# W_in centred and row sums scaled when added; every second tile of x read as columns from a second, transposed layout

## The chip, the core and the metric

The kernel runs on one core of a Trainium2 chip. The metric is the device time of one execution in microseconds (us). Before: median 858.76 us of three runs (858.76, 859.01, 854.37).

## What is computed

With `ln` a layer norm without weights and `rms(v, g)` = v / sqrt(mean(v^2) + 1e-5) * g:

```
h  = rms(ln(x), g_res) @ W_in.T + b_in
x1 = x + h + depool(rms(ctx, g_init)[:, :512])[plug]
y  = x1 + gelu(ln(x1) @ w1 + b1) @ w2 + b2
```

x is 4096 x 512, ctx 3202 x 1024, w1 512 x 2048, all fp32. `depool` is a first-order recurrence over the rows of the context (a scan); `plug` picks a scanned row for each row of x and is worked out from the mask by integer sums.

## The kernel before

The rows of x are 32 tiles of 128 rows; four tiles make a group of 512 rows (8 groups). Each fp32 product is formed as three fp32r products of high and low parts (`split_product`, L780 to L783): hi\*hi, hi\*lo, lo\*hi. A high part is a ScalarE copy into fp32r, a low part the difference of the value and its high part.

**First stage**, one tile after another (`t` from 0 to 31 on every engine). SyncE loads the tile into one of 16 slots (`xa`). VectorE takes its statistics (`tile_stats`, L927, L928), POOL turns them into scale and bias (`scales`, L470 to L473), ScalarE normalizes (`tile_norm`, L634, into `n_rows`), TensorE transposes in four pieces (`transpose_first`, L776) into one of three PSUM banks, ScalarE forms the high part (`tile_high`, L641), VectorE the low part (`tile_low`, L932), and TensorE multiplies with W_in (`project`, 12 matmuls of 128x512). VectorE adds the product to x in the slot (`tile_add`, L938), and SyncE stores x1 to memory (`store_x1`, L359). High and low parts have four slots (`HB`), the products three banks. W_in is split once at the start, scaled by g_res (`high_w_in`, `low_w_in`).

Between the tiles, at slots written out by hand (`if t == ...`), stand the integer work on the mask (`mask_parts` to `mask_rows`, `one_hots_p`, `one_hots_q`, `count_rows`, `finish_plug` on VectorE; `mask_totals`, `count_positions`, `count_before` on TensorE), the first two blocks of the context scan (`squares`, `times_g_init`, `scale_rows`, `scan_row`, `carry` L800, `add_carry`), which are stored in a table in memory, and for group 0 the reload of x1 (`x_next`), `add_bias`, the gathers from the table (`add_context`, L510) on POOL, the second layer norm (`second_stats`, `group_scale`, `second_norm` L1057) and its transposes (`transpose_second`, L824). POOL forms the low parts of w1 and w2 (`low_w1` L478, `low_w2` L484).

**Second stage**, 8 groups: for m from 0 to 15, `ffn1` (12 matmuls), twice Gelu on ScalarE, the low part on VectorE (L1144) and two steps later `ffn2` (12 matmuls); the scan blocks 2 to 6 and the preparation of the next group lie beside it. Each engine executes its own instructions in the order in which they are written; semaphores connect them.

## Time and profile before

| | |
|---|---|
| timed runs | 858.76, 859.01, 854.37 us; median 858.76 |
| the profiled execution | 854.02 us |
| its span, first to last instruction | 851.9 us |
| TensorE matmul busy | 827.5 us, 97% of the span, 3758 instructions |
| VectorE, ScalarE, POOL busy | 315.2, 293.1, 267.8 us |
| moved by DMA | 73.17 MB |
| granted TensorE clock, mean | 0.998 |

The page cuts the span into 40 slices of 21.3 us; TensorE is at nine tenths or more in all but the first and the last two or so. In rows of the profile PE is TensorE, PEld its weight loads, DVE VectorE, ACT ScalarE, POOL GpSimd; SPq and ACTq are the queues on which SyncE and ScalarE issue DMAs. A busy time of a matmul overlaps the next one's; steps from start to start tell its length better.

### The profile page before, as it was taken

Reading aid. Unit: us, or ns where it says so; the run is one execution under the profiler, and the core shown is the slowest. Engines: PE = TensorE matmul, PEld = TensorE weight load, DVE = VectorE, ACT = ScalarE, POOL = GpSimd, SP = SyncE. Lnnn points to the kernel's source line nnn. Section 1 sums busy time; section 2 is a strip of 40 time slices with the busy share of each in tenths; the row PEclk is TensorE's granted clock in tenths of the full one; section 3 lists DMA queues with packets and bytes.
Section 4 is the critical chain, followed back from the end, with each engine's and each line's share of the span. In section 5 each row is a group of like instructions: output and inputs, shape, how many; then the busy total and the mean of one; then the engine's idle time right before and its main releaser. Section 6 shows DMA issues by size and latency. Waiting matters only on the chain.

```text
span 851.9 us, 10840 instructions
## 1 busy us (share of the span) xinstructions
PE 827.5 (97%) x3758; PEld 679.9 (80%) x3758; DVE 315.2 (37%) x523; ACT 293.1 (34%) x506; POOL 267.8 (31%) x290
## 2 busy tenths in 40 slices
PE   4998999999999999999999999999999999999998
PEld 3776788788888888888888887888888888888886
DVE  5888862444342242414151424234113311241112
ACT  4674535542532235222622243223222322222221
POOL 6263666970162005310522044202500250011000
PEclk9999999999999999999999999999999999999999
DMA  9876798160214212241125021402300140010001
GB/s 235 278 212 189 249 240 307 50 165 7 75 50 122 49 49 74 72 99 38 43 82 132 0 74 49 97 0 95 53 1 1 50 89 9 0 49 1 1 1 49
DMA packets 35688, 73.17 MB, mean 86 GB/s; under 512 B 5796, under 2 KB 5796, under 8 KB 33768
## 3 DMA queue, kind: packets, MB, share of 16 engines
q1 hardware_dynamic: 26972, 61.54, 22.1%
q0 software_dynamic: 4608, 8.39, 6.2%
q10 hardware_dynamic: 4080, 2.89, 1.2%
q8 instruction: 14, 0.23, 0.1%
q14 instruction: 14, 0.11, 0.0%
HBM read 48.92 MB, written 23.89 MB: 85 GB/s over the span
## 4 chain that ended last, share of the span: by engine, by line
PE 86%; DVE 4%; POOL 4%; issue 2%; ACT 2%; DMA 1%; SPq 0%; POOLq 0%; DVEq 0%; ACTq 0%
PE acc L781 14%; PE acc L782 14%; PE acc L783 14%; PE h_bank L781 13%; PE h_bank L783 13%; PE h_bank L782 13%; PE t_bank L824 2%; DVE cl L944 1%; PE t_bank L776 1%; DMA x_next<-x_part 1%; POOL w_lo L478 1%; POOL cl L497 1%; POOL w_lo L484 1%; POOL x_next L505 1%; DMA xa_even<-in_x_dram 1%
## 5 line engine op out<-in xcount | busy, mean ns | idle before, releaser
L1144 DVE TENSOR_TENSOR h_lo<-g_f,h_hi 128x512 fp32r<-128x512 f32 x128 | 100.9, 788 | 452.0 <-ACT g_f L728 452.0
L726 ACT ACTIVATE h_hi<-h_bank,b_c 128x512 fp32r<-128x512 f32 x128 | 88.1, 688 | 434.4 <-PE h_bank L783 429.6
L781 PE MATMUL h_bank<-xt_hi,w_hi 128*128 128x512 f32 x512 | 201.9, 394 | 0.0
L781 PE MATMUL acc<-w_hi,h_hi 128*128 128x512 f32 x512 | 199.8, 390 | 0.0
L783 PE MATMUL h_bank<-xt_hi,w_lo 128*128 128x512 f32 x512 | 199.4, 389 | 0.0
L782 PE MATMUL h_bank<-xt_lo,w_hi 128*128 128x512 f32 x512 | 199.3, 389 | 0.0
L783 PE MATMUL acc<-w_hi,h_lo 128*128 128x512 f32 x512 | 199.2, 389 | 0.0
L782 PE MATMUL acc<-w_lo,h_hi 128*128 128x512 f32 x512 | 199.2, 389 | 0.0
L782 PEld LDWEIGHTS h_bank<-xt_lo,w_hi 128*128 128x128 f32 x512 | 96.2, 188 | 20.8 <-issue 1.2
L781 PEld LDWEIGHTS h_bank<-xt_hi,w_hi 128*128 128x128 f32 x512 | 96.1, 188 | 20.8 <-issue 1.2
L783 PEld LDWEIGHTS h_bank<-xt_hi,w_lo 128*128 128x128 f32 x512 | 96.1, 188 | 20.1
L783 PEld LDWEIGHTS acc<-w_hi,h_lo 128*128 128x128 f32 x512 | 96.1, 188 | 20.0
L781 PEld LDWEIGHTS acc<-w_hi,h_hi 128*128 128x128 f32 x512 | 96.1, 188 | 19.7
L782 PEld LDWEIGHTS acc<-w_lo,h_hi 128*128 128x128 f32 x512 | 96.1, 188 | 19.6
L728 ACT ACTIVATE g_f<-h_bank,b_c 128x512 f32<-128x512 f32 x128 | 87.4, 683 | 0.0
L510 POOL DMA_INDIRECT x_next<-scan_table,idx x32 | 51.3, 1602 | 65.9 <-DMA scan_table<-cl 55.9
L497 POOL TENSOR_TENSOR cl<-cl,g_init_b 128x512 f32<-128x512 f32 x24 | 31.3, 1313 | 97.2 <-ACT ch L646 96.9
L571 POOL TENSOR_TENSOR x_cur<-x_next,b_b 128x512 f32<-128x512 f32 x32 | 43.5, 1390 | 56.3 <-DMA out_dram<-x_cur 55.9
L515 POOL TENSOR_SCALAR va_b<-mv_b 128x4 f32<-128x4 f32 x8 | 1.6, 196 | 187.2 <-DVE mv_b L1048 187.2
L505 POOL TENSOR_TENSOR x_next<-x_next,b_in_b 128x512 f32<-128x512 f32 x32 | 46.3, 1446 | 33.8 <-DMA x_next<-x_part 30.2
L781 PE MATMUL acc<-win_hi,h_hi 128*128 128x512 f32 x88 | 38.1, 434 | 0.0
L783 PE MATMUL acc<-win_hi,h_lo 128*128 128x512 f32 x88 | 34.9, 396 | 0.0
(145 smaller groups left out, 706.3 us busy)
## 6 DMA issues: line engine op xcount, KB each, us to landing
x_next<-x_part SPq DMA_DIRECT2D x8, 1024.0 KB, 4.8
out_dram<-x_cur SPq DMA_DIRECT2D x32, 256.0 KB, 2.1
w_raw<-in_L_ffn_w_dram SPq DMA_DIRECT2D x6, 1024.0 KB, 9.0
scan_table<-cl SPq DMA_DIRECT2D x6, 896.0 KB
ch<-in_ctx_dram SPq DMA_DIRECT2D x20, 256.0 KB, 2.9
cl<-in_ctx_dram SPq DMA_DIRECT2D x5, 1024.0 KB
xa_even<-in_x_dram SPq DMA_DIRECT2D x16, 256.0 KB, 5.2
xa_odd<-in_x_dram SPq DMA_DIRECT2D x16, 256.0 KB, 5.7
```

What stands on the lines that cost most here:

```text
L478: pool.tensor_tensor(w_lo[:, k, r], w_raw[:, k, r], w_hi[:, k, r].bitcast(F32), ALU.subtract).then_inc(w1_ready, 1)
L497: pool.tensor_tensor(rows[:, j, :], rows[:, j, :], g_init_b[:], ALU.mult).then_inc(g_scaled, 1)
L505: step(pool.tensor_tensor(x_next[:, i, :], x_next[:, i, :], b_in_b[:], ALU.add))
L510: pool.indirect_dma_start(x_next[:, i, :], None, rows, bass.IndirectOffsetOnAxis(ap=idx[:, i:i + 1].bitcast(U32), axis=0), compute_op=ALU. ...
L571: ins = pool.tensor_tensor(x_cur[:, i, :], x_next[:, i, :], b2_b[:], ALU.add)
L726: act.activation(h_hi[:, m % HB, :], h_bank[m % 2][:], ACT.Gelu, bias=b1_c[:, m:m + 1])
L728: act.activation(g_f32[:], h_bank[m % 2][:], ACT.Gelu, bias=b1_c[:, m:m + 1]).then_inc(gelu_done, 1)
L781: nc.tensor.matmul(dst, a_hi, b_hi, start=first, stop=False)
L782: nc.tensor.matmul(dst, a_hi, b_lo, start=False, stop=False)
L783: return nc.tensor.matmul(dst, a_lo, b_hi, start=False, stop=final)
L824: ins = nc.tensor.transpose(t_bank[i % 2][:, k * P:(k + 1) * P], n_rows[:, i, k * P:(k + 1) * P], ident[:])
L1144: dve.tensor_tensor(h_lo[:, m % HB, :], g_f32[:], h_hi[:, m % HB, :].bitcast(F32), ALU.subtract).then_inc(h_split, 1)
```

## The change

1. **Normalization moves behind the product.** TensorE transposes x as it was loaded. W_in is scaled by g_res and each column is centred: four plain fp32 matmuls (`sum_w_in`) with `g_wide`, a 128-column copy of g_res, give the column sums in every row of a bank, and VectorE subtracts 1/512 of them (`centre_w_in`). The product is scaled by the row's factor when it is added (`tile_add` becomes a `scalar_tensor_tensor`). `tile_norm` and two of POOL's four scale operations go.
2. **Odd tiles from 3 on** (15 of 32) are not transposed. The host passes `x_cols`, x with rows and columns of each tile exchanged; SyncE loads it beside the tile into an unused part of `w_raw` (`xc`, 12 slots). Their low part is formed on POOL (`tile_low`).
3. **Around it**: the first four x1 tiles stay in `x_next` and are neither stored nor loaded again; POOL's `add_bias`, gathers, `low_w1`, half of `low_w2` and `group_scale` for group 0 get slots between the tiles; POOL's two clearings of `cl` and `ch_all` go to VectorE; two of the four W_in loads are issued by ScalarE; on TensorE `mask_totals`, `count_before` and the first carry come one tile earlier, and on VectorE most of the mask work and parts of the scan too.

```diff
@@ -95,7 +95,17 @@
-def xattn_ffn(nc, x, ctx, mask, w_in, b_in, g_res, g_init, w1, b1, w2, b2, out):
+def from_host(t):
+    return t % 2 == 1 and t >= 3
+TURNED = [t for t in range(NT) if not from_host(t)]
+HOSTED = [t for t in range(NT) if from_host(t)]
+XTR = 12
+def xattn_ffn(nc, x, x_cols, ctx, mask, w_in, b_in, g_res, g_init, w1, b1, w2, b2, out):
@@ -176,10 +187,28 @@
+        def xc(t):
+            u = HOSTED.index(t) % XTR
+            q = 3 - u // K
+            return w_raw[:, u % K, q * D:(q + 1) * D]
+        def turned_bank(t):
+            return first_bank[TURNED.index(t) % 3]
+        def x1(t):
+            return x_next[:, t, :] if t < TI else xa(t)
@@ -306,9 +341,9 @@
+            for k in range(2, K):
+                sp.dma_start(win_raw[:, k, :], win_v[:, k, :]).then_inc(win_loaded[k], 16)
...
-            for k in range(K):
-                sp.dma_start(win_raw[:, k, :], win_v[:, k, :]).then_inc(win_loaded[k], 16)
@@ -316,6 +351,11 @@
+                if from_host(t):
+                    m = HOSTED.index(t)
+                    if m >= XTR:
+                        wait_apart(sp, xc_lo, m - XTR + 1)
+                    sp.dma_start(xc(t), x_cols[t, :, :]).then_inc(xc_loaded[m % XTR], 16)
@@ -374,19 +414,15 @@
-                if t > 0:
+                if t > TI:
...
-                    if loaded >= XR:
+                    if XR <= loaded < XR + TI:
+                        wait_apart(sp, acc_read, loaded - XR + 1)
+                    if loaded >= XR + TI:
...
-                if t == 17:
-                    wait_apart(sp, plug_ready, 1)
-                    for j in range(TI):
-                        wait_x1(j)
-                    sp.dma_start(x_next[:], x1_dram[0, :, :, :]).then_inc(x_next_loaded, 16)
@@ -467,10 +504,14 @@
+                if t0 > 0:
+                    pool.wait_ge(ra_ready, t0)
...
-                step(pool.tensor_tensor(ra[:, u], va_a[:, 0:n], neg_half[:, 0:n], ALU.pow))
-                step(pool.tensor_tensor(mr_a[:, 0:n], mv_a[:, u, 0], ra[:, u], ALU.mult))
-                pool.tensor_scalar(na_bias[:, u], mr_a[:, 0:n], -1.0, 1.0, ALU.mult, ALU.mult).then_inc(ra_ready, n)
+                pool.tensor_tensor(ra[:, u], va_a[:, 0:n], neg_half[:, 0:n], ALU.pow).then_inc(ra_ready, n)
+            def tile_low(t):
+                pool.wait_ge(x_hi, t + 1)
+                pool.tensor_tensor(h_lo[:, t % HB, :], xc(t), h_hi[:, t % HB, :].bitcast(F32), ALU.subtract).then_inc(xc_lo, 1)
@@ -515,41 +556,47 @@
-            pool.memset(cl[:], 0.0).then_inc(zeroed, 1)
-            pool.memset(ch_all[:], 0.0).then_inc(zeroed, 1)
-            for t in range(4):
-                scales(t, 1)
+            scales(0, 2)
+            scales(2, 2)
...
-            scales(4, 2)
...
+                if t + 2 < NT and from_host(t + 2):
+                    tile_low(t + 2)
...
-                if t == 18:
-                    pool.wait_ge(plug_ready, 1)
-                    gather_indices(0)
-                    pool.wait_ge(x_next_loaded, 16)
-                    for i in range(TI):
-                        add_bias(i)
-                if t % 2 == 0 and t + 6 < NT:
-                    scales(t + 6, 2)
+                if t % 4 == 2 and t + 2 < NT:
+                    scales(t + 2, TI)
...
-            wait_apart(pool, table_stored, STORED + BLOCK_STORED * 2)
-            for i in range(TI):
-                add_context(0, i, 2)
-            for k in range(K):
-                low_w1(0, k, 1)
-            group_scale(0)
+                if 14 <= t <= 17:
+                    pool.wait_ge(acc_read, t - 13)
+                    add_bias(t - 14)
+                if t == 18:
+                    pool.wait_ge(plug_ready, 1)
+                    gather_indices(0)
+                if t in (23, 24):
+                    if t == 23:
+                        wait_apart(pool, table_stored, STORED + BLOCK_STORED * 2)
+                    add_context(0, 2 * (t - 23), 2)
+                    add_context(0, 2 * (t - 23) + 1, 2)
+                if t in (25, 26):
+                    low_w1(0, 2 * (t - 25), 1)
+                    low_w1(0, 2 * (t - 25) + 1, 1)
+                if t == 27:
+                    low_w2(0, 0, 2)
+                    low_w2(0, 1, 2)
+                if t == 28:
+                    group_scale(0)
...
-            for q in range(4):
+            for q in range(2, 4):
@@ -622,23 +671,19 @@
-            def tile_norm(t):
-                act.wait_ge(ra_ready, t + 1)
-                if t >= TI:
-                    act.wait_ge(t_done, t - TI + 1)
-                u = t % XR
-                act.activation(n_rows[:, t % TI, :], xa(t), ACT.Identity, bias=na_bias[:, u:u + 1],
-                               scale=ra[:, u:u + 1]).then_inc(n_ready, 1)
...
-                act.wait_ge(t_done, t + 1)
...
-                act.activation(h_hi[:, t % HB, :], first_bank[t % 3][:], ACT.Copy).then_inc(t_hi, 1)
+                if from_host(t):
+                    m = HOSTED.index(t)
+                    act.wait_ge(xc_loaded[m % XTR], 16 * (m // XTR) + 16)
+                    act.activation(h_hi[:, t % HB, :], xc(t), ACT.Copy).then_inc(x_hi, 1)
+                else:
+                    act.wait_ge(x_turned, TURNED.index(t) + 1)
+                    act.activation(h_hi[:, t % HB, :], turned_bank(t)[:], ACT.Copy).then_inc(x_hi, 1)
@@ -654,34 +699,28 @@
-            def high_w_in(k):
+            for k in range(K):
+                act.activation(g_wide[:, k, :], ones[:], ACT.Copy, scale=g_res_c[:, k:k + 1]).then_inc(g_made, 1)
+            for k in range(K):
...
-                act.activation(win_hi[:, k, :], win_raw[:, k, :], ACT.Copy, scale=g_res_c[:, k:k + 1]).then_inc(win_hi_done, 1)
-            high_w_in(0)
-            high_w_in(1)
-            tile_norm(0)
-            high_w_in(2)
+                act.activation(win_g[:, k, :], win_raw[:, k, :], ACT.Copy, scale=g_res_c[:, k:k + 1]).then_inc(win_scaled, 1)
...
-            high_w_in(3)
-            tile_norm(1)
+            for k in range(K):
+                act.wait_ge(win_centred, k + 1)
+                act.activation(win_hi[:, k, :], win_raw[:, k, :], ACT.Copy).then_inc(win_hi_done, 1)
...
-            tile_norm(2)
...
-                if t + 3 < NT:
-                    tile_norm(t + 3)
@@ -769,13 +808,21 @@
-                pe.wait_ge(n_ready, t + 1)
-                if t >= 3:
-                    pe.wait_ge(t_lo, t - 2)
+                pe.wait_ge(xa_loaded[t % XR], 16 * (t // XR) + 16)
+                n = TURNED.index(t)
+                if n >= 3:
+                    pe.wait_ge(x_lo, n - 2)
...
-                    ins = nc.tensor.transpose(first_bank[t % 3][:, k * P:(k + 1) * P],
-                                              n_rows[:, t % TI, k * P:(k + 1) * P], ident[:])
-                ins.then_inc(t_done, 1)
+                    ins = nc.tensor.transpose(turned_bank(t)[:, k * P:(k + 1) * P], xa(t)[:, k * P:(k + 1) * P], ident[:])
+                ins.then_inc(x_turned, 1)
+            def sum_w_in():
+                for k in range(K):
+                    pe.wait_ge(g_made, k + 1)
+                    pe.wait_ge(win_loaded[k], 16)
+                    ins = nc.tensor.matmul(acc[3][:], g_wide[:, k, :], win_raw[:, k, :], start=(k == 0), stop=(k == K - 1))
+                ins.then_inc(win_summed, 1)
@@ -783,7 +830,10 @@
-                pe.wait_ge(t_lo, t + 1)
+                if from_host(t):
+                    pe.wait_ge(xc_lo, HOSTED.index(t) + 1)
+                else:
+                    pe.wait_ge(x_lo, TURNED.index(t) + 1)
@@ -819,26 +869,27 @@
+            sum_w_in()
...
-            for t in range(3):
-                project(t)
-                transpose_first(t + 2)
-            for t in range(3, NT):
-                if t + 2 < NT:
+            for t in range(NT):
+                if t + 2 < NT and not from_host(t + 2):
...
-                if t == 3:
+                if t == 2:
...
+                if t == 14:
+                    count_before()
...
-                    count_before()
-                if t == 16:
@@ -928,14 +981,16 @@
-                dve.wait_ge(t_hi, t + 1)
-                dve.tensor_tensor(h_lo[:, t % HB, :], first_bank[t % 3][:], h_hi[:, t % HB, :].bitcast(F32),
-                                  ALU.subtract).then_inc(t_lo, 1)
+                dve.wait_ge(x_hi, t + 1)
+                dve.tensor_tensor(h_lo[:, t % HB, :], turned_bank(t)[:], h_hi[:, t % HB, :].bitcast(F32),
+                                  ALU.subtract).then_inc(x_lo, 1)
...
-                dve.tensor_tensor(xa(t), p_bank[t % 3][:], xa(t), ALU.add).then_inc(acc_read, 1)
+                dve.wait_ge(ra_ready, t + 1)
+                u = t % XR
+                dve.scalar_tensor_tensor(x1(t), p_bank[t % 3][:], ra[:, u:u + 1], xa(t), ALU.mult, ALU.add).then_inc(acc_read, 1)
@@ -1014,13 +1069,18 @@
-            def low_w_in(ks):
-                dve.wait_ge(g_res_loaded, 16)
-                for k in ks:
-                    dve.wait_ge(win_hi_done, k + 1)
-                    dve.scalar_tensor_tensor(win_lo[:, k, :], win_raw[:, k, :], g_res_c[:, k:k + 1], win_hi[:, k, :].bitcast(F32),
-                                             ALU.mult, ALU.subtract).then_inc(win_lo_done, 1)
+            def centre_w_in(k):
+                if k == 0:
+                    dve.wait_ge(win_summed, 1)
+                dve.wait_ge(win_scaled, k + 1)
+                dve.scalar_tensor_tensor(win_raw[:, k, :], acc[3][:], -1.0 / D, win_g[:, k, :], ALU.mult, ALU.add)\
+                    .then_inc(win_centred, 1)
+            def low_w_in(k):
+                dve.wait_ge(win_hi_done, k + 1)
+                dve.tensor_tensor(win_lo[:, k, :], win_raw[:, k, :], win_hi[:, k, :].bitcast(F32),
+                                  ALU.subtract).then_inc(win_lo_done, 1)
@@ -1050,63 +1110,64 @@
-            low_w_in((0, 1))
-            tile_stats(1)
-            low_w_in((2,))
...
-            low_w_in((3,))
-            tile_stats(2)
-            tile_stats(3)
+            centre_w_in(0)
+            centre_w_in(1)
+            low_w_in(0)
+            centre_w_in(2)
+            low_w_in(1)
+            centre_w_in(3)
+            low_w_in(2)
+            low_w_in(3)
...
-            tile_stats(4)
-            tile_stats(5)
+            for t in range(1, 6):
+                tile_stats(t)
...
@@ -1203,8 +1264,11 @@
+    laid = dict(inputs)
+    laid['L0_xattn_W_in'] = _np.asarray(inputs['L0_xattn_W_in']).T
+    laid['x_cols'] = _np.asarray(inputs['x']).reshape(NG, P, TI, K, P).transpose(0, 2, 4, 3, 1).reshape(NT, P, D)
...
-        a = _np.ascontiguousarray(inputs[name].T if name == 'L0_xattn_W_in' else inputs[name])
+        a = _np.ascontiguousarray(laid[name])
...
```

TensorE's order at the start, before (`n_rows` are the normalized rows, `win_hi` and `win_lo` the parts of W_in):

```order
L776 MATMUL t_bank<-ident,n_rows 128x128 [waits n_ready,consts_made]
L776 MATMUL t_bank<-ident,n_rows 128x128 x3
L776 MATMUL t_bank<-ident,n_rows 128x128 [waits n_ready]
L776 MATMUL t_bank<-ident,n_rows 128x128 x3
L781 MATMUL acc<-win_hi,h_hi 128x512 [waits win_lo_done,win_hi_done,t_lo]
L782 MATMUL acc<-win_lo,h_hi 128x512
L783 MATMUL acc<-win_hi,h_lo 128x512
L781 MATMUL acc<-win_hi,h_hi 128x512 [waits win_lo_done,win_hi_done]
```

and with the change (`g_wide` is g_res over 128 columns):

```order
L816 MATMUL t_bank<-ident,xa_even 128x128 [waits xa_loaded0,consts_made]
L816 MATMUL t_bank<-ident,xa_even 128x128 x3
L824 MATMUL acc<-win_raw,g_wide 128x512 [waits win_loaded0,g_made]
L824 MATMUL acc<-win_raw,g_wide 128x512 [waits win_loaded1,g_made]
L824 MATMUL acc<-win_raw,g_wide 128x512 [waits win_loaded2,g_made]
L824 MATMUL acc<-win_raw,g_wide 128x512 [waits win_loaded3,g_made]
L816 MATMUL t_bank<-ident,xa_even 128x128 [waits xa_loaded1]
L816 MATMUL t_bank<-ident,xa_even 128x128 x3
L816 MATMUL acc<-ident,xa_even 128x128 [waits xa_loaded2]
L816 MATMUL acc<-ident,xa_even 128x128 x3
L828 MATMUL acc<-win_hi,h_hi 128x512 [waits win_lo_done,win_hi_done,x_lo]
L829 MATMUL acc<-win_lo,h_hi 128x512
```

The transposes wait for a load instead of normalized rows; four fp32 products stand between tile 0 and tile 1, and tile 2 is transposed ahead of the first product.

VectorE's order from the low part of tile 0 (L985; L1077 centres, L1082 forms the low part of W_in, L980 and L981 are the statistics) to the second of the five statistics, with the change:

```order
L985 TENSOR_TENSOR h_lo<-t_bank,h_hi 128x512 [waits x_hi]
L1077 SCALAR_TENSOR_TENSOR win_raw<-acc,win_g 128x512 [waits win_scaled,win_summed]
L1077 SCALAR_TENSOR_TENSOR win_raw<-acc,win_g 128x512 [waits win_scaled]
L1082 TENSOR_TENSOR win_lo<-win_raw,win_hi 128x512 [waits win_hi_done]
L1077 SCALAR_TENSOR_TENSOR win_raw<-acc,win_g 128x512 [waits win_scaled]
L1082 TENSOR_TENSOR win_lo<-win_raw,win_hi 128x512 [waits win_hi_done]
L1077 SCALAR_TENSOR_TENSOR win_raw<-acc,win_g 128x512 [waits win_scaled]
L1082 TENSOR_TENSOR win_lo<-win_raw,win_hi 128x512 [waits win_hi_done] x2
L985 TENSOR_TENSOR h_lo<-t_bank,h_hi 128x512 [waits x_hi]
L980 BN_STATS st_a<-xa_even 128x6 [waits xa_loaded1]
L981 BN_AGGR mv_a<-st_a 128x2 [waits dve_self]
```

All that concerns W_in waits for `win_summed`, TensorE's sums. Three more statistics follow, then the low part of tile 2 and the mask's work. Before, the same stretch was:

```order
L1022 SCALAR_TENSOR_TENSOR win_lo<-win_raw,g_res_c,win_hi 128x512 [waits win_hi_done,g_res_loaded]
L1022 SCALAR_TENSOR_TENSOR win_lo<-win_raw,g_res_c,win_hi 128x512 [waits win_hi_done]
L927 BN_STATS st_a<-xa_even 128x6 [waits xa_loaded1]
L928 BN_AGGR mv_a<-st_a 128x2 [waits dve_self]
L1022 SCALAR_TENSOR_TENSOR win_lo<-win_raw,g_res_c,win_hi 128x512 [waits win_hi_done,g_res_loaded]
L932 TENSOR_TENSOR h_lo<-t_bank,h_hi 128x512 [waits t_hi]
L1022 SCALAR_TENSOR_TENSOR win_lo<-win_raw,g_res_c,win_hi 128x512 [waits win_hi_done,g_res_loaded]
L927 BN_STATS st_a<-xa_even 128x6 [waits xa_loaded2]
L928 BN_AGGR mv_a<-st_a 128x2 [waits dve_self]
L927 BN_STATS st_a<-xa_even 128x6 [waits xa_loaded3]
L928 BN_AGGR mv_a<-st_a 128x2 [waits dve_self]
L932 TENSOR_TENSOR h_lo<-t_bank,h_hi 128x512 [waits t_hi]
```

There, two statistics stand between the low part of W_in and that of tile 1, and two more before that of tile 2.

POOL's order from the gathers of group 0 (L551) to the scale of the group (L557), with the change (L514 is the low part of a tile from the host, L519 and L525 those of w1 and w2):

```order
L551 DMA x_next<-scan_table,idx 128x512 [waits table_stored]
L551 DMA x_next<-scan_table,idx 128x512 x3
L514 TENSOR_TENSOR h_lo<-w_raw,h_hi 128x512 [waits x_hi]
L519 TENSOR_TENSOR w_lo<-w_raw,w_hi 128x512 [waits w_hi_done] x2
L509 TENSOR_SCALAR va_a<-mv_a 128x4 [waits mv_a_ready,ra_ready]
L510 TENSOR_TENSOR ra<-va_a,neg_half 128x4 [waits pool_self]
L519 TENSOR_TENSOR w_lo<-w_raw,w_hi 128x512 [waits w_hi_done] x2
L514 TENSOR_TENSOR h_lo<-w_raw,h_hi 128x512 [waits x_hi]
L525 TENSOR_TENSOR w_lo<-w_raw,w_hi 128x512 [waits w_hi_done] x2
L556 TENSOR_SCALAR va_b<-mv_b 128x4 [waits mv_b_ready]
L557 TENSOR_TENSOR rb<-va_b,neg_half 128x4 [waits pool_self]
L514 TENSOR_TENSOR h_lo<-w_raw,h_hi 128x512 [waits x_hi]
```

The low parts of tiles 27, 29 and 31 (L514) now stand between the gathers and the other work; before, POOL did only scale and bias for the tiles, and the gathers came behind the last of them.

## Rows read from the trace of the kernel before

**Rows 1.** Stretches: us, busy time and instructions of each engine, clock, DMA share, GB/s.

```profile
26.50:130.60 104.10, 98.57 (x505) 79.78 (x504) 82.55 (x170) 55.87 (x99) 55.55 (x85) 0.98 0.76 230
...
209.90:299.80 89.90, 89.85 (x402) 73.93 (x402) 29.93 (x44) 30.04 (x56) 26.17 (x23) 1.00 0.24 70
...
60.00:80.00 20.00, 16.83 (x76) 12.77 (x75) 14.81 (x35) 10.69 (x19) 9.87 (x19) 0.91 0.72 217
```

**Rows 2.** Timeline of TensorE: start, us, engine, line, operation.

```profile
26.56 0.47 PE L781 MATMUL acc<-win_hi,h_hi 128*128 128x512 f32 x1
...
130.62 0.39 PE L781 MATMUL h_bank<-xt_hi,w_hi 128*128 128x512 f32 x1
...
133.34 0.39 PE L781 MATMUL h_bank<-xt_hi,w_hi 128*128 128x512 f32 x1
```

**Rows 3.** Chain of waits, in order of time: start us, us, what.

```profile
74.42 1.11 PE t_bank L776 x4
75.53 1.71 PE acc L800 x2
...
107.50 0.44 PE t_bank L776 x4
110.71 0.44 PE t_bank L776 x4
...
255.32 0.86 PE t_bank L800 x2
```

**Rows 4.** Timeline of TensorE: its waits in the projection [idle before <-releaser].

```profile
56.88 0.66 PE L776 MATMUL acc<-ident,n_rows 128*128 128x128 f32 x4 [1.69 <-ACT n_rows L634]
...
74.42 1.11 PE L776 MATMUL t_bank<-ident,n_rows 128*128 128x128 f32 x4 [2.92 <-ACT n_rows L634]
...
97.67 0.66 PE L776 MATMUL t_bank<-ident,n_rows 128*128 128x128 f32 x4 [0.67 <-ACT n_rows L634]
```

**Rows 5.** VectorE, one line each: count, min/median/max ns, first and last start.

```profile
L944 DVE SCALAR_TENSOR_TENSOR cl<-cl x18: 683/1666/1787, 65.5 to 523.9; 128x512 f32<-128x512 f32 x18
...
L938 DVE TENSOR_TENSOR xa_even<-acc,xa_even x11: 657/658/692, 20.3 to 101.4; 128x512 f32<-128x512 f32 x11
```

**Rows 6.** Timeline of the start: VectorE, and issues on ScalarE's queue.

```profile
5.32 0.69 DVE L927 BATCH_NORM_STATS2 st_a<-xa_even 128x6 f32<-128x512 f32 x1 [4.31 <-DMA xa_even<-in_x_dram]
...
8.86 0.70 DVE L927 BATCH_NORM_STATS2 st_a<-xa_even 128x6 f32<-128x512 f32 x1 [0.39 <-DMA xa_even<-in_x_dram]
...
11.97 0.35 ACTq L675 DMA_DIRECT2D g_init_b<-in_L_xattn_g_init_dram  x1
...
12.61 0.69 DVE L927 BATCH_NORM_STATS2 st_a<-xa_even 128x6 f32<-128x512 f32 x1
...
13.39 0.66 ACTq L676 DMA_DIRECT2D b_c<-in_L_ffn_b_dram  x1
...
13.50 0.66 DVE L927 BATCH_NORM_STATS2 st_a<-xa_even 128x6 f32<-128x512 f32 x1
...
22.63 0.17 DVE L960 TENSOR_SCALAR part_i<-mask_i 128x26 int32<-128x26 int32 x1
...
24.23 0.17 DVE L973 COPY part_f<-cum_f 128x3 f32<-128x3 f32 x1
```

**Rows 7.** Timeline at the end of the projection: SyncE's queue, POOL, VectorE.

```profile
96.50 0.82 SPq L344 DMA_DIRECT2D scan_table<-cl_next  x2
...
104.03 1.82 POOL L510 DMA_INDIRECT x_next<-scan_table,idx  x1 [0.69 <-issue]
...
110.84 5.62 POOL L478 TENSOR_TENSOR w_lo<-w_raw,w_hi 128x512 fp32r<-128x512 f32 x4
...
121.18 1.04 POOL L516 TENSOR_TENSOR rb<-va_b,neg_half 128x4 f32<-128x4 f32 x1
...
122.32 1.92 DVE L1057 TENSOR_SCALAR n_rows<-x_next,mv_b,rb 128x512 f32<-128x512 f32 x4 [0.20 <-POOL rb L516]
```

**Rows 8.** DMA issues: KB each, us from issue to landing.

```profile
b_c<-in_L_ffn_b_dram ACTq DMA_DIRECT2D x1, 8.0 KB, 22.3
```

107 lines of the change are left out of this document (62 added, 45 removed).

## The prediction

> **What bounds the kernel now.** I read the stretches first. In a feed-forward group TensorE is busy 89.85 of 89.90 us; the projection of the first 32 tiles, 26.5 to 130.6 us, has 98.57 of 104.10 [rows 1]. So time can be won where the projection waits, where TensorE does work that can be left out, or in the start; the feed-forward groups keep all their matmuls.
>
> Then TensorE's timeline [rows 2] and the chain of waits [rows 3]. Twelve matmuls, one tile's product, take 133.34 - 130.62 = 2.72 us. A tile with its four transposes takes 110.71 - 107.50 = 3.21 us. The transposes cost 0.49 us per tile. The projection of tile 3 begins at 26.56 and the first feed-forward matmul at 130.62: 104.1 us for 29 tiles, of which 29 x 2.72 = 78.9 are products, 26 x 0.49 = 12.7 transposes. Waits on the normalized rows take 1.7, 2.9 and 0.7 us [rows 4]. Behind the second one the granted clock is low (0.91 over 60 to 80 us [rows 1], its lower level of 1.2 GHz for part of that stretch): the carry there takes 1.71 where another takes 0.86, and the four transposes 1.11 where others take 0.44 [rows 3, 4]. That is 1.5 us more, so the waits cost 5.3 + 1.5 = 6.8 us. The rest of the 104.1, some 5.7 us, is the first transposes of the feed-forward, the carries and counts.
>
> **The change, part by part.**
>
> *Transposes.* Of the 26 sets issued after the projection of tile 3, thirteen go (tiles 7, 9, ... 31): 13 x 0.49 = 6.4 us on the bounding engine. The transposes that stay read x as loaded, so statistics, scales and normalization no longer stand ahead of them. All three long waits name the normalized rows [rows 4]; I take all 6.8 us as gained and nothing, if another wait follows in their place, as the lower end. What is late next is the high and low parts, which need one ScalarE pass and one VectorE or POOL pass, with three tiles of lead; and the addition, which now needs the scale. VectorE loses 15 low-part subtractions, about 0.66 us each by the nearest operation of that shape with one operand in PSUM [rows 5], so it has more air; ScalarE loses 32 passes. That is hidden either way, and worth nothing beyond the waits. The store and reload of the first four x1 tiles go too: they were beside other work.
>
> Together: -6.4 - 6.8 = **-13.2 us** between the projection of tile 3 and the feed-forward.
>
> *Start.* This part gets dearer. The first load landed at 5.3 us and the sixth at 8.9, so 0.7 us each [rows 6]. Tile 0 is now about third of five loads on two queues: 6.7 to 7.3, I take 7.0. Its transposes take 1.1 us at the lower clock [rows 3]. Then come four plain fp32 products of W_in with a row of g: 0.86 us each at 2.4 GHz, 1.71 at 1.2 GHz, by the carry, the same kind and size [rows 3]. The bounds are 3.4 and 6.8; I take two at either level, 5.1, and reach 13.2. Only then can VectorE centre the four pieces and form their low parts: eight operations of 0.6 to 0.7 us, one ScalarE pass exposed at the end, 5.5 us: 18.7. ScalarE issues four small loads before the high part of tile 1: from 11.97 to 14.05, 2.1 us [rows 6]. They begin at about 17.4, so that high part ends near 20.1 and the low part near 20.8.
>
> Behind it VectorE now has five statistics before the low part of tile 2: 5 x 0.89 (13.50 - 12.61) = 4.5. With the low part 25.9, and with the mask's integer work, which TensorE now needs one tile earlier and which takes 24.4 - 22.6 = 1.8 us [rows 6], 27.6. TensorE, done with tile 1 near 23.5, waits some 4 us, longer than the 2.9 us behind which the clock fell above; so I add 1.5 us as there. The product of tile 3 begins at 27.8 + 2.7 + 1.5 = 32.0, against 26.56: **+5.4 us**. Lower end +3 (all sums at 2.4 GHz, clock kept), upper end +8 (all at 1.2 GHz, loads 1 us later).
>
> *POOL at the end of the projection.* POOL executes in order, and the low parts of the tiles from the host stand between its gathers and the low parts of w1 and w2. The table's last store was issued by 97.3, and the first gather began at 104.03: 6.7 us at most [rows 7]. The second block's carry is placed as before, so the store goes at about 90 and gathers begin by 96.5, four in 6.8 us (104.03 to 110.84) until 103.3. A subtraction takes 5.62 / 4 = 1.4 [rows 7]: the low part of tile 27 is there at 104.7, its product due at 32.0 + 24 x 2.72 + 12 x 0.49 + 3 = 106. Four subtractions for w1, four scales and tile 29 come next: 104.7 + 5.6 + 1.2 + 1.4 = 112.9, due at 111.9: 1 us late. Two more subtractions, then the scale of the group (1.4 us from 120.83 to 122.2), then the first normalized row (1.92 / 4) [rows 7]: 117.6, where TensorE, 1 us behind already, wants it at 115.6: 3 us late in all. But 6.7 us is an upper bound, since POOL had other work between that store and its gather; with a table 2 us sooner 1 us is left, with one 3 us sooner nothing, and where POOL meets VectorE at the port 4 us. I take the middle of 3 and 1, **+2.0 us**, bounds 0 and 4.
>
> *The port.* The same VectorE operation on two SBUF operands takes 683 ns at least and 1666 ns at the median [rows 5]; most of the slow ones lie in the groups in which POOL forms low parts of the weights. The additions, with one operand in PSUM, take 657 to 692 ns throughout [rows 5]; they and the low parts, of the same kind, are most of what VectorE does here. The Trainium skill, "SBUF — State Buffer", section "SBUF: two separate sides", says that a VectorE instruction with two SBUF inputs and a POOL instruction hold the shared port in turn, each for its whole length; it speaks against putting subtractions on POOL. By that rule the six scan rows behind tiles 12 to 16, which met no POOL work before, may each wait. The sum takes nothing for it; the third case below does.
>
> Sum: -13.2 + 5.4 + 2.0 = **-5.8 us**. Against the profiled execution, 854.02 us with a span of 851.9, that is 848.2. The three timed runs have a median of 858.76, and of the four executions two are near 854 and two near 859. I expect the same spread after, so I start from the mean of the four, 856.5, and forecast **851 us** (856.5 - 5.8 = 850.7).
>
> **The cases.**
>
> 1. *The sum holds*, -4.3 to -8: 0.52.
>
> 2. *The start costs less*: the clock stays up and the sums end sooner, +3, and POOL is in time, 0: -10.2 us, 846. For it: behind the wait of 1.7 us the four transposes took 0.66 us and not the 1.11 they took behind 2.9 us [rows 4], so the clock holds through the shorter kind. Against it: five statistics stand ahead of tile 2 whatever the clock does. 0.15.
>
> 3. *The port and POOL give back the gain.* Six scan rows of 1.67 instead of 0.68 are 6 us on VectorE between tiles 12 and 16, with about 3 us of lead: TensorE waits 3 us more at the two carries. That gives -2.8, or 854, within 0.5% (4.3 us, about what a measurement of this kernel can tell from no change). For it: the spread in [rows 5], and POOL's 15 new subtractions. Against it: they meet only where both happen to run. 0.20.
>
> 4. *Slower: POOL blocked by a small load.* From tile 5 on POOL waits for four small loads before it scales the context. The last one took 22.3 us from its issue [rows 8]; issued near 19 instead of 13.4 it lands at 41. Behind that wait stand two context rows, four scales and the low part of tile 9: 5.2 us, 46.5, due at about 50. So it decides from a landing at 45 on, and one at 58, if 15 extra loads on the other queue hold it back, would cost 13 us: -5.8 + 13 = +7, or 864. Against it: the extra loads of that time are 1.5 MB less the 1 MB of x1 stores that go. With any other cause of a gain turned into a loss above 4.3 us it gets 0.13.
>
> So faster 0.67, same 0.20, slower 0.13. The range: 844 is case 2 with the lower two executions of four; 858 takes in the worst ends of case 3 and leaves out case 4: 0.8 inside.
>
> **What would show it.** In the profile after: twelve-matmul tiles alternate 2.72 and 3.21 us with no wait over 1 us from tile 3 to 26; the first matmul of tile 3 lies near 32 us, behind a wait of some 4 us on the mask's totals or the low part of tile 2; a wait of 1 to 3 us before the transposes of the feed-forward, released by POOL or by the normalized rows; feed-forward groups of 89.9 us as before; the first feed-forward matmul near 124.8. I am wrong if that matmul comes after 128, or if TensorE waits for the low parts of tiles from the host before tile 27. If the feed-forward groups change length, the sum is wrong at a place that it holds fixed.

## The result, and the profile after

The changed kernel takes 860.97 us (median of 12 runs, 857.82 to 863.14), the kernel before 856.24 us in the same comparison: ratio 1.0051, 95% interval 1.0036 to 1.0067. It is 4.7 us or 0.5% slower; the forecast was 851 us, and 860.97 lies above its range of 844 to 858.

The profiled execution took 862.8 us with a span of 861.0, against 854.02 and 851.9 before. This pair lies further apart than the medians: 862.8 is among the longest executions after, 854.02 is shorter than any of the twelve before. Four marks on TensorE's timeline cut the 9.1 us between these two into pieces:

| from the span's start, us | before | after | longer by |
|---|---|---|---|
| product of tile 3 begins | 26.56 | 33.58 | +7.0 |
| from there to the product of tile 26 | 84.35 | 75.52 | -8.8 |
| from there to the first feed-forward matmul | 19.71 | 28.77 | +9.1 |
| from there to the end of the span | 721.3 | 723.1 | +1.8 |

So the middle gained as it should in kind, the start cost about what was expected, and 9 us were lost between tile 26 and the feed-forward, where the forecast had 1.0 (2.0 for POOL, less two sets of transposes).

The stretches of the kernel after (stretch: us, then busy time and instructions of PE, PEld, DVE, ACT, POOL, then granted clock, DMA share, GB/s):

```profile
33.50:137.80 104.30, 94.73 (x451) 75.96 (x451) 82.55 (x154) 35.99 (x72) 64.80 (x61) 0.97 0.74 227
219.10:309.00 89.90, 89.83 (x403) 73.90 (x402) 30.14 (x44) 29.99 (x56) 26.15 (x23) 1.00 0.24 70
20.00:40.00 20.00, 14.99 (x63) 11.71 (x62) 16.95 (x39) 4.99 (x11) 8.32 (x14) 0.91 0.87 265
40.00:60.00 20.00, 17.89 (x84) 14.22 (x83) 18.86 (x38) 11.71 (x30) 14.49 (x14) 1.00 0.51 137
60.00:80.00 20.00, 19.55 (x115) 15.83 (x115) 19.00 (x36) 9.24 (x20) 15.94 (x17) 1.00 0.93 337
80.00:100.00 20.00, 19.16 (x89) 15.20 (x88) 18.91 (x36) 6.43 (x8) 7.90 (x9) 1.00 0.80 231
```

The first two rows answer to [rows 1]. The projection is as long as before (104.3 us) with 3.8 us less of TensorE's work in it; the feed-forward group has not moved. In the third column of busy times (DVE), VectorE works 19 of every 20 us from 40 to 100. Before, the stretch from 60 to 80 had 14.81 [rows 1]. It has no air left, though it lost 15 subtractions. Before, it was nearly as full on either side of that stretch:

```profile
40.00:60.00 20.00, 18.31 (x114) 14.99 (x113) 18.30 (x34) 14.76 (x34) 12.44 (x18) 1.00 0.68 187
...
80.00:100.00 20.00, 19.34 (x95) 15.44 (x94) 18.55 (x36) 10.05 (x14) 10.10 (x20) 1.00 0.73 253
```

What TensorE waited for from 20 to 150 us (engine, tile and line, then the releaser, whose work ended the wait: us, times, longest):

```profile
PE h_bank L855 <- DVE part_f L1028: 4.2, 1, 4.2
PE acc L828 <- POOL h_lo L514: 3.7, 1, 3.7
PE t_bank L877 <- DVE n_rows L1115: 2.4, 1, 2.4
PE h_bank L828 <- DVE xa_odd L993: 1.3, 1, 1.3
PE h_bank L850 <- DVE cl_next L999: 0.8, 1, 0.8
```

The three waits of [rows 4] are gone. In their place stand the mask's totals (4.2), the low part of tile 27 on POOL (3.7), and the normalized rows of the first feed-forward group (2.4). Behind each of these three the granted clock falls to the lower level for part of the next 20 us, to a mean of 0.91, or some 1.8 us lost each time.

The chain of waits shows what stood behind the last two (start us, us, what; in order of time):

```profile
99.98 0.37 SPq L384
...
100.39 5.74 DMA scan_table<-cl_next
...
107.05 1.28 POOL x_next L551
...
112.88 1.54 POOL x_next L551
114.42 1.30 POOL h_lo L514
115.72 2.45 POOL w_lo L519 x2
...
119.64 2.51 POOL w_lo L519 x2
122.15 1.25 POOL h_lo L514
123.40 0.44 POOL w_lo L525
...
126.32 1.01 POOL rb L557
...
127.43 1.43 DVE n_rows L1115
...
128.91 1.92 PE t_bank L877 x8
```

The table's last store is issued at 99.98, where [rows 7] have 96.50, and the first gather begins at 107.05 instead of 104.03. VectorE ended its last addition of the carry at 97.03; the store came 2.9 us later because it stands in SyncE's queue behind that of an x1 tile, whose addition ended at 99.45. Before, it was 93.65, and the same 2.9 us. Behind the four gathers POOL has two low parts of tiles, six low parts of weights and two scales in one queue. TensorE is at that time waiting for POOL, not leading it.

Why VectorE is full is seen in its timeline and POOL's at the same time (start, us, engine, line, operation). VectorE:

```profile
73.67 0.68 DVE L985 TENSOR_TENSOR h_lo<-t_bank,h_hi 128x512 fp32r<-128x512 f32 x1
74.27 0.15 DVE L1096 COPY grp<-h_bank 128x8 f32<-128x8 f32 x1
74.46 0.17 DVE L1097 TENSOR_TENSOR_SCAN fa<-one_row,grp 128x8 f32<-128x8 f32 x1
74.67 1.22 DVE L1098 TENSOR_TENSOR fa<-fa,grp 128x8 f32<-128x8 f32 x1
75.92 0.16 DVE L1099 TENSOR_TENSOR fa<-fa,h_bank 128x8 f32<-128x8 f32 x1
76.12 1.22 DVE L1100 TENSOR_TENSOR plug_f<-cnt,fa 128x32 f32<-128x32 f32 x1
77.37 1.20 DVE L1101 TENSOR_SCALAR plug<-plug_f 128x32 int32<-128x32 f32 x1
```

POOL:

```profile
74.57 1.29 POOL L546 TENSOR_TENSOR x_next<-x_next,b_in_b 128x512 f32<-128x512 f32 x1
76.01 1.29 POOL L514 TENSOR_TENSOR h_lo<-w_raw,h_hi 128x512 fp32r<-128x512 f32 x1
77.25 1.29 POOL L546 TENSOR_TENSOR x_next<-x_next,b_in_b 128x512 f32<-128x512 f32 x1
```

The same three operations before (L1038, L1040, L1041 there):

```profile
74.70 0.17 DVE L1038 TENSOR_TENSOR fa<-fa,grp 128x8 f32<-128x8 f32 x1
...
75.10 0.19 DVE L1040 TENSOR_TENSOR plug_f<-cnt,fa 128x32 f32<-128x32 f32 x1
75.32 0.18 DVE L1041 TENSOR_SCALAR plug<-plug_f 128x32 int32<-128x32 f32 x1
```

Each of these operations on 8 or 32 columns starts during a POOL instruction of 1.29 us and ends when that one ends: 74.67 + 1.22 = 75.89 against 74.57 + 1.29 = 75.86. Eight operations on 8 to 32 columns took 1.2 us instead of 0.2 in the kernel after, one in the kernel before: some 7 us more on VectorE. Four of the eight met the low part of a tile (L514). The other four met POOL's multiplications with g_init (L538) and additions of b_in (L546), which the kernel before has too, at other times.

### The profile page after: what moved, and what is told of

The parts are those of the page before. It is cut to its first block, busy times and chain, and to the rows that moved or that the text cites. A ratio compares the mean times of both kernels' runs of the same rounds, so it can differ in the third digit from the quotient of the medians.

```text
span 861.0 us, 10600 instructions
## 1 busy us (share of the span) xinstructions
PE 831.4 (97%) x3706; PEld 678.6 (79%) x3706; DVE 322.4 (37%) x514; ACT 272.5 (32%) x482; POOL 270.9 (31%) x249
## 4 chain that ended last, share of the span: by engine, by line
PE 81%; DVE 10%; POOL 2%; issue 2%; DMA 2%; ACT 2%; SPq 0%; ACTq 0%; DVEq 0%; POOLq 0%
PE acc L828 13%; PE acc L829 13%; PE acc L830 13%; PE h_bank L828 13%; PE h_bank L829 13%; PE h_bank L830 13%; PE t_bank L877 2%; DVE st_a L980 2%; DVE cl L999 1%; DVE h_lo L985 1%; DMA ch<-in_ctx_dram 1%; DVE xa_even L993 1%; POOL x_next L551 1%; PE acc L824 1%; DMA scan_table<-cl_next 1%
## 5 line engine op out<-in xcount | busy, mean ns | idle before, releaser
L828 PEld LDWEIGHTS h_bank<-xt_hi,w_hi 128*128 128x128 f32 x512 | 96.5, 188 | 20.9 <-issue 1.2
L551 POOL DMA_INDIRECT x_next<-scan_table,idx x32 | 50.9, 1590 | 71.8 <-DMA scan_table<-cl 57.7
L538 POOL TENSOR_TENSOR cl<-cl,g_init_b 128x512 f32<-128x512 f32 x24 | 30.9, 1292 | 102.8 <-ACT ch L691 97.6
L546 POOL TENSOR_TENSOR x_next<-x_next,b_in_b 128x512 f32<-128x512 f32 x32 | 46.5, 1453 | 30.6 <-DMA x_next<-x_part 27.3
```

The costliest lines, as they stand in the source:

```text
L538: pool.tensor_tensor(rows[:, j, :], rows[:, j, :], g_init_b[:], ALU.mult).then_inc(g_scaled, 1)
L546: step(pool.tensor_tensor(x_next[:, i, :], x_next[:, i, :], b_in_b[:], ALU.add))
L551: pool.indirect_dma_start(x_next[:, i, :], None, rows, bass.IndirectOffsetOnAxis(ap=idx[:, i:i + 1].bitcast(U32), axis=0), compute_op=ALU. ...
L828: nc.tensor.matmul(dst, a_hi, b_hi, start=first, stop=False)
```

## The experiments

All are edits of the changed kernel, each compared with the kernel before on the same chip. The chip isn't the same for all: the medians of the kernel before lie between 855.05 and 857.31 us in these comparisons, so runs are best held against each other by their ratios. This table has the marks of the profiled executions and the ratio to the kernel before. A mark is that of one execution: with the same work ahead of it on TensorE and VectorE, tile 3 begins at 33.58 in the kernel after and at 32.33 in e1, where the four sums took 4.98 us and not 6.10.

| run | product of tile 3 | product of tile 26 | first gather | feed-forward | median us | ratio (95%) |
|---|---|---|---|---|---|---|
| before | 26.56 | 110.91 | 104.03 | 130.62 | | |
| after | 33.58 | 109.10 | 107.05 | 137.87 | 860.97 | 1.0051 (1.0036-1.0067) |
| e1_late_dve | 32.33 | 107.84 | 105.75 | 134.74 | 858.94 | 1.0032 (1.0007-1.0057) |
| e2_all_dve | 32.39 | 112.02 | 109.14 | 137.24 | 857.86 | 1.0043 (1.0019-1.0067) |
| e3_no_host | 32.82 | 109.31 | 105.75 | 133.28 | 855.82 | 1.0003 (0.9983-1.0024) |
| e4_no_centre | 23.53 | 104.40 | 101.59 | 130.81 | 854.21 | 0.9985 (0.9967-1.0004) |
| e5_early_stats | 27.41 | 102.50 | 99.94 | 130.75 | 853.68 | 0.9969 (0.9949-0.9989) |
| e6_early_late_scale | 28.34 | 103.87 | 101.28 | 128.25 | 853.35 | 0.9955 (0.9937-0.9972) |
| e7_turned_early_scale | 28.21 | 104.78 | 101.18 | 127.56 | 850.03 | 0.9920 (0.9904-0.9937) |
| e8_extra_pool | 27.05 | 105.19 | 101.77 | 128.28 | 852.28 | 0.9948 (0.9929-0.9967) |
| e9_short_turned | 27.51 | 103.98 | 96.08 | 126.34 | 850.74 | 0.9918 (0.9889-0.9946) |
| e10_short_hosted | 26.78 | 100.72 | 95.29 | 122.59 | 846.41 | 0.9868 (0.9832-0.9903) |
| e11_defer_only | 23.26 | 99.83 | 95.89 | 122.42 | 848.44 | 0.9902 (0.9865-0.9939) |
| e12_table_ahead | 27.07 | 107.55 | 100.49 | 129.40 | 851.85 | 0.9958 (0.9941-0.9974) |
| e13_gathers_between | 28.09 | 103.65 | 95.38 | 125.52 | 849.33 | 0.9915 (0.9886-0.9943) |

### e1_late_dve: the last three low parts on VectorE

```diff
+def on_pool(t):
+    return from_host(t) and t < 27
-                if t + 2 < NT and from_host(t + 2):      # POOL
+                if t + 2 < NT and on_pool(t + 2):
-                if t + 2 < NT and not from_host(t + 2):  # VectorE
+                if t + 2 < NT and not on_pool(t + 2):
```

> The changed kernel, with the low parts of tiles 27, 29 and 31 on VectorE and not on POOL (12 of 15 stay on POOL). Theory A (POOL's order at the end: these low parts stand behind the wait for the table and the four gathers): the wait of about 3.3 us ahead of the product of tile 27 and the slow clock behind it go, and the later wait gets shorter; the first feed-forward matmul comes at 130 to 132 us, not 137.9, and the time is 853 to 856 us, not 861. Rival B (the table itself is late because VectorE is behind, so the second wait, for the scale of the group, takes the whole place of the first): the first feed-forward matmul stays at 135 or later, time 858 or more.

Measured: 858.94 us. The wait of 3.7 us at tile 27 is gone, and another has grown:

```profile
PE t_bank L894 <- DVE n_rows L1132: 5.7, 1, 5.7
```

The feed-forward comes 3.1 us earlier, not 6 to 8, and 1.25 us of that were there at tile 3 already, which the edit does not touch. The time is as rival B gave it, the mark 0.3 us short of its 135. POOL's late low parts cost about 2 us; behind them stands the same chain of table, gathers, scale and normalized rows.

### e2_all_dve: all low parts on VectorE

The same edit with `on_pool` always false: POOL has no low parts of tiles.

> The changed kernel, with the low parts of all 15 tiles from the host on VectorE. Theory C (the port: VectorE's operations on 26 columns, 1.2 us instead of 0.18, sit behind POOL's subtractions): at most two of them stay above 1 us, which gives VectorE 6 to 7 us back, about what the 12 low parts before 100 us cost it; tile 26 starts at about 109 us as before, and with the waits at the end gone the time is 853 to 857 us. Rival D (these operations are slow for a cause of their own, or behind POOL's other work): at least six stay at 1.2 us, VectorE has 8 us more to do, tile 26 starts at 114 us or later, and the time stays at 860 or above.

Measured: 857.86 us, four slow small operations, gathers at 109.14. Both theories missed. VectorE got some 11 subtractions more before the table (11 x 0.6 = 6.6 us) and lost four slow operations (4 us); the gathers came 2.1 us later. VectorE's own load moves the table. The profiled execution, 862.09 us, is one of the four of ten that took over 861, so these marks are later than those of a middling one.

### e3_no_host: nothing from the second layout

```diff
 def from_host(t):
-    return t % 2 == 1 and t >= 3
+    return False
```

> The changed kernel without tiles from the host: all 32 are loaded once and transposed on TensorE, low parts on VectorE; the deferred normalization and the centred W_in stay. TensorE gets 15 x 0.49 = 7.3 us more, POOL 15 subtractions less. Theory A with C: the two waits at the end (6 us and 3 us of slow clock) go, so the time comes to 857 to 860 us. Rival D (VectorE alone is the bound from 20 to 100 us and now has 10 us more): 864 us or more.

Measured: 855.82 us, better than either theory gave and equal to the kernel before. TensorE does all 13 sets of transposes again, 6.4 us of work, and the feed-forward comes 4.6 us earlier than with the second layout. So in this order the second layout costs 4 to 5 us (1.0051 against 1.0003). Its saving is nowhere on the path, and what it put on POOL is.

### e4_no_centre: no sums, no centring

```diff
-            sum_w_in()
...
-                act.activation(win_hi[:, k, :], win_raw[:, k, :], ACT.Copy)
+                act.activation(win_hi[:, k, :], win_raw[:, k, :], ACT.Copy, scale=g_res_c[:, k:k + 1])
```

This leaves the row mean out of the normalization.

> The changed kernel without the centring of W_in: no column sums, W_in is scaled and split straight from its load (the mean of a row is not taken out of the product). Theory S (the four plain fp32 products and the chain behind them cost the start 6 to 7 us that nothing hides): the product of tile 3 begins at 26 to 28 us, not 33.6, and the time falls by 5 to 7 us to about 855. Rival E (VectorE is the bound from 20 to 100 us whatever the start does, and only its own work counts; or the wait for the table at the end takes the gain): less than 2.5 us reach the end, 858.5 or above.

Measured: 854.21 us, the time as theory S gave it, tile 3 earlier than it did (23.53, not 26 to 28). Tile 3 begins 10 us earlier, tile 26 only 4.7 us. TensorE now waits 3.5 us for VectorE's additions instead: the head start runs into VectorE's queue. This gave the next theory (V): VectorE's load from 20 us to the table sets the table, and table, gathers and scale set the feed-forward.

### e5_early_stats: VectorE's work moved into its own gap

```diff
             tile_stats(0)
+            tile_stats(1)
             tile_low(0)
+            tile_stats(2)
+            mask_parts()
             centre_w_in(0)
...
-            for t in range(1, 6):
-                tile_stats(t)
...
                 if t == 0:
-                    mask_parts()
+                    for i in range(3, 6):
+                        tile_stats(i)
```

> The changed kernel, with 4.5 us of VectorE's work (the statistics of tiles 1 and 2 and the mask's integer work) moved into the 6 us in which VectorE waits for the sums of W_in. Theory V (VectorE has no air from 20 to 105 us, so what it does there sets the table and, through the gathers, the end): the product of tile 3 begins near 27 rather than 33.6, the gathers begin near 102 rather than 107, the first feed-forward matmul comes at 131 to 134, and the time is 854 to 857. Theory R (the start is only a start: the rest of the projection waits for other things, as where the centring was left out and 10 us at tile 3 became 5 at tile 26): the gathers begin after 105, the feed-forward after 135.5, the time is 858.5 or more.

Measured: 853.68 us, 0.8% under the kernel after, with nothing else touched. VectorE at the start:

```profile
10.79 0.68 DVE L980 BATCH_NORM_STATS2 st_a<-xa_even 128x6 f32<-128x512 f32 x1
...
11.67 0.15 DVE L1015 TENSOR_SCALAR part_i<-mask_i 128x26 int32<-128x26 int32 x1
...
13.26 0.17 DVE L1028 COPY part_f<-cum_f 128x3 f32<-128x3 f32 x1
14.02 1.29 DVE L1077 SCALAR_TENSOR_TENSOR win_raw<-acc,win_g 128x512 f32<-128x512 f32 x2 [0.59 <-PE acc L824]
```

The statistics and the mask's work fit ahead of the sums' end at no cost. Everything that follows is 6 to 7 us earlier, to the gathers (99.94) and the feed-forward (130.75), each a little earlier than theory V gave it. Theory V holds, and theory R does not.

### e6_early_late_scale: late low parts on VectorE, scale ahead of the weights

On top of e5 and e1, POOL does the scale of the first group before six low parts of weights:

```diff
-                if t in (25, 26):
-                    low_w1(0, 2 * (t - 25), 1)
-                    low_w1(0, 2 * (t - 25) + 1, 1)
-                if t == 27:
-                    low_w2(0, 0, 2)
-                    low_w2(0, 1, 2)
                 if t == 28:
                     group_scale(0)
+                    for k in range(K):
+                        low_w1(0, k, 1)
+                    low_w2(0, 0, 2)
+                    low_w2(0, 1, 2)
```

> The kernel of the run before this one, with the low parts of tiles 27, 29 and 31 on VectorE, and with the scale of the first feed-forward group ahead of the six low parts of weights on POOL. Theory P (at the end the chain is gathers, statistics, scale, normalization, and each subtraction that stands in POOL's queue between gathers and scale makes it longer): the wait on the normalized rows, 5.7 us with the late low parts alone on VectorE, falls under 3, the first feed-forward matmul comes 2 to 4 us earlier than without this, and the time is 851 to 854. Theory Q (the landing of the gathers sets the statistics, whatever POOL does behind them): the scale comes less than 1 us earlier against the landing of the fourth gather, and the time is 855 or more.

Measured: 853.35 us. The feed-forward comes 2.5 us before that of e5, as theory P had it, but the longest wait on the normalized rows is 3.2 us. POOL now stands idle before the scale, and VectorE before the last statistics:

```profile
107.11 1.54 POOL L568 DMA_INDIRECT x_next<-scan_table,idx  x1 [0.30 <-issue]
...
115.74 0.20 POOL L573 TENSOR_SCALAR va_b<-mv_b 128x4 f32<-128x4 f32 x1 [5.63 <-DVE mv_b L1123]
```

```profile
114.60 0.69 DVE L1122 BATCH_NORM_STATS2 st_b<-x_next 128x6 f32<-128x512 f32 x1 [1.48 <-DMA x_next<-scan_table,idx]
```

So the gathers' own landing, 7.5 us from the fourth one's issue to 114.60, and the statistics are part of what is left of that chain (Q). Another part comes with the edit itself. The low parts of the weights now run while VectorE normalizes, and its four operations take 1.41 to 1.50 us, where three of the four took 0.54 in the kernel after:

```profile
117.08 5.50 POOL L536 TENSOR_TENSOR w_lo<-w_raw,w_hi 128x512 fp32r<-128x512 f32 x4
...
L1130 DVE TENSOR_SCALAR n_rows<-x_next,mv_b,rb x4: 1408/1486/1499, 117.2 to 121.4; 128x512 f32<-128x512 f32 x4
```

TensorE waits 0.75 us for the second row behind the 3.2 for the first. It is so in every run with the early scale (1.43 to 1.51 us in e13); no run puts these low parts behind the normalization. The time did not follow: the span from the first feed-forward matmul to the end is 723.4 us here and 721.3 in e5. Here the clock fell in group 0 behind a wait of 2.3 us for the carry (a mean of 0.91 from 160 to 180); in e5 it stayed up behind 1.8.

### e7_turned_early_scale: the same without the second layout

> All tiles turned by TensorE, nothing from the second layout, with the same early VectorE work and the early scale. Theory V: without the second layout VectorE has 15 subtractions more, 10 us, but meets no subtractions of POOL; the waits at the start and the end go, so the projection runs at 3.2 us a tile from 27 on and the feed-forward starts at 127.5 to 130: 850 to 853. Theory H (the transposes that the second layout saves are worth their 6.4 us once nothing else is late): this kernel is 3 us or more behind the run before this one.

Measured: 850.03 us, 0.8% below the kernel before, as theory V gave it: the fastest kernel that computes everything, with e13. The stretch from tile 3 to the feed-forward:

```profile
28.20:127.50 99.30, 97.02 (x505) 78.97 (x504) 89.28 (x172) 37.71 (x73) 48.84 (x48) 1.00 0.73 218
```

TensorE is busy 97.0 of 99.3 us at full clock. The centred W_in and the deferred scales make the transposes independent of the statistics, and that gain shows once VectorE's gap is used and POOL's scale is early; how much each of the two gives here was not separated.

### e8_extra_pool: POOL's subtractions alone, put back

```diff
+                if t % 2 == 1 and t + 2 < 27:
+                    pool.wait_ge(x_hi, t + 3)
+                    pool.tensor_tensor(w_raw[:, 0, 3 * D:4 * D], w_raw[:, 1, 3 * D:4 * D],
+                                       w_raw[:, 1, 3 * D:4 * D], ALU.subtract).then_inc(xc_lo, 1)
```

> The kernel with all tiles turned, early VectorE work and early scale (850.03 us), with twelve subtractions of 128x512 added on POOL, at the places where the low parts of the tiles from the host stood, on data that nobody uses. Nothing waits for them but POOL's own queue. Theory C (a small VectorE operation of 26 columns that meets such a subtraction takes 1.2 us rather than 0.2): six or more of them are slow where that kernel has three, VectorE's queue comes out 3 to 6 us later, the gathers begin at 104 to 107 rather than 101.2, and the time is 852 to 856. Theory D (POOL's subtractions cost VectorE nothing that counts, VectorE's own work alone decides): the gathers stay within 1 us of 101.2 and the time is 849.5 to 851.

Measured: 852.28 us, and the gathers 0.6 us later. Four small operations over 0.9 us instead of two:

```profile
68.45 1.22 DVE L1099 TENSOR_TENSOR fa<-fa,grp 128x8 f32<-128x8 f32 x1
...
69.90 1.04 DVE L1101 TENSOR_TENSOR plug_f<-cnt,fa 128x32 f32<-128x32 f32 x1
70.98 1.21 DVE L1102 TENSOR_SCALAR plug<-plug_f 128x32 int32<-128x32 f32 x1
```

The time is just inside what theory C gave, the gathers are where theory D had them. The extra collisions are there, but the traces do not show that they cost the 2 us: the feed-forward begins 0.7 us later than in e7, and the other 2.3 us between the two spans (851.7 and 848.7) lie behind it, where the clock fell in group 0 behind a wait of 1.9 us and not behind e7's 1.8. The subtractions also lengthen POOL's own queue. Which operations meet is a matter of phase. The intervals of e7 and e8 just overlap.

### e9_short_turned and e10_short_hosted: less of the scan ahead of the table

```diff
-                ins = dve.scalar_tensor_tensor(rows[:, j, :], rows[:, j - 1, :], A, rows[:, j, :], ...)
+                c = slice(0, 32 if isinstance(b, int) and b < NA else D)
+                ins = dve.scalar_tensor_tensor(rows[:, j, c], rows[:, j - 1, c], A, rows[:, j, c], ...)
```

Both do the scan rows, and the additions of the carry, of the first two blocks on 32 of 512 columns, which leaves out the rest of that part of the scan. e9 is e7 with this, e10 is e6 with it.

> The kernel with all tiles turned, early VectorE work and early scale, with the scan rows and the additions of the carry of the first two context blocks done on 32 of 512 columns: it leaves the rest of that part of the scan out, 14 operations and some 8.5 us of VectorE's work before the table. TensorE's work is as it was, 3.2 us a tile. Theory V (the table and the gathers set the start of the feed-forward, through VectorE): gathers near 93, the product of tile 26 at 104.5 as before (TensorE had few waits there), the first feed-forward matmul at 124 to 125, as soon as TensorE is through: 846 to 848. Theory T (TensorE is what bounds already): less than 1 us is gained.

> The same shortened scan, in the kernel that has every second tile from the second layout, the low parts of tiles 27, 29 and 31 on VectorE, early VectorE work and early scale (853.35 us with the full scan). Theory V (the 6.4 us of transposes that the second layout saves are there, but VectorE and the table hide them): the product of tile 26 comes at 97 to 100, the first feed-forward matmul 3 us or more before that of the run with all tiles turned and the same short scan, and the time is 841 to 845, lower than that run. Theory H (the second layout saves nothing, or its low parts on POOL cost as much as it saves): not faster than that run, 846 or more.

Measured: 850.74 and 846.41 us. With all tiles turned, 8.5 us less on VectorE and gathers 5 us earlier gain nothing against e7 (theory T there): TensorE bounds it at 3.2 us a tile. With the second layout the same cut takes e6's 853.35 to 846.41, and the feed-forward comes 3.75 us before that of e9. So the saved transposes are real (4.3 us of 6.4), and they are hidden as long as the table is late. That is theory V in kind; the time is 1.4 us above what it gave, and the product of tile 26 0.7 us.

### e11_defer_only: the price of centring in the better order

e7 without sums and centring; it leaves the row mean out.

> All tiles turned, normalization deferred, early mask work and early scale, but W_in not centred and no column sums: it leaves the row mean out of the normalization. Against the same kernel with the centring (850.03 us). Theory S (the centring costs its 5 us at the start, and the start is carried to the end because VectorE's queue begins earlier too): the product of tile 3 near 22 to 24 rather than 28.2, gathers at 96 to 98 rather than 101.2, feed-forward at 122 to 124, time 845 to 847. Theory E (VectorE has to do the work anyway, and only fills in the time in which it waited for the sums): tile 3 early, but gathers after 99.5 and the time 848.5 or more.

Measured: gathers at 95.89 and feed-forward at 122.42, 5 us before e7 as theory S had it, but a median of 848.44 us over four runs from 845.62 (the profiled one) to 850.28. The trace says 5 us, the medians 1.6 with overlapping intervals. What the other three runs lost is open.

### e12_table_ahead and e13_gathers_between: the table earlier with the whole scan

```diff
                 if t == 17:
-                    add_carry(0, acc[3][:], cl, (0, 1))
+                    add_carry(0, acc[3][:], cl, range(R))
                 if t == 18:
-                    add_carry(0, acc[3][:], cl, (2, 3))
+                    add_carry(1, h_bank[0][:], cl_next, range(R))
...
-                if t == 19:
+                if t == 17:
                     store_block(0, cl)
-                if t == 21:
+                if t == 18:
                     store_block(1, cl_next)
```

e12 also puts the statistics of tiles 23 to 31 behind the carries. e13 leaves them, and has POOL issue the gathers at tiles 22 and 23, not 23 and 24.

> The kernel with every second tile from the second layout, late low parts on VectorE, early VectorE work and early scale (853.35 us), and with the whole scan kept: VectorE adds both carries at tiles 17 and 18 instead of 17 to 20, the statistics of tiles 23 to 31 come behind them, and the two blocks of the table are stored at tiles 17 and 18 of SP's queue instead of 19 and 21. Nothing is left out or saved on any engine. Theory V (the table decides when the second layout's 6 us show): the gathers begin at 92 to 97 instead of 101.3, the first feed-forward matmul comes at 121.5 to 124.5 instead of 128.25, as with the short scan, and the time is 845 to 849, below the 850.03 us of the kernel with all tiles turned. Theory W (VectorE has no air, so work put ahead only makes the tiles' additions late and TensorE waits for them): the gathers come earlier, but the feed-forward begins after 126 and the time is 850.5 or more.

> The same as the run before this one (whole scan, table stored at tiles 17 and 18), but the statistics stay where they were in the changed kernel, so POOL's scale for tiles 20 to 23 doesn't wait 10.6 us for them, and POOL issues two gathers ahead of the low part of tile 25 and two behind it, instead of all four behind. Theory V (the table and the gathers decide when the second layout's saving shows): the gathers begin at 92 to 97, the product of tile 26 comes at 102 to 104.5, the first feed-forward matmul at 121.5 to 125, and the time is 845 to 849. Theory W (VectorE has no air, work put ahead on it comes back as a wait of TensorE): the product of tile 26 comes after 105.5, the feed-forward after 126.5, and the time is 850.5 or more.

Measured: 851.85 and 849.33 us. In e12 POOL waited for the late statistics, and the low parts of two tiles with it:

```profile
88.06 0.19 POOL L526 TENSOR_SCALAR va_a<-mv_a 128x4 f32<-128x4 f32 x1 [10.59 <-DVE mv_a L996]
...
99.02 1.30 POOL L531 TENSOR_TENSOR h_lo<-w_raw,h_hi 128x512 fp32r<-128x512 f32 x1 [4.86 <-ACT h_hi L698]
100.49 1.81 POOL L568 DMA_INDIRECT x_next<-scan_table,idx  x1 [0.18 <-issue]
```

The first gather began at 100.49, right behind a low part and with no wait for the table. By its marks and its time e12 came out as theory W gave it. In e13, without that wait, the gathers begin at 95.38 and the feed-forward at 125.52, 2.7 us before e6 and 2.0 before e7. The time is 849.33 us, 4 us under e6; against e7 the intervals overlap. The gathers and tile 26 are as theory V gave them, the feed-forward and the time 0.5 and 0.3 us past its bounds; none of them reached those of W. Of the 4.9 us between the spans of e6 and e13, 2.7 lie before the feed-forward and 2.2 behind it, where e6's clock fell in group 0. e13 is the fastest version with the second layout that computes everything, and 0.85% faster than the kernel before.

## Why the prediction was wrong

*The step that failed* is in one sentence: "The second block's carry is placed as before, so the store goes at about 90 and gathers begin by 96.5". They began at 107.05, 10.5 us later. The place in the program is as before, but it is a place in VectorE's queue, and that queue came there late. From tile 3 to the end of the last addition of the carry passed 67.1 us before (26.56 to 93.65) and 63.5 us after (33.58 to 97.03), 3.6 less. With tile 3 forecast 5.4 us later and the store 6.5 us earlier, the sentence takes this stretch to be 12 us shorter. The feed-forward, forecast near 124.8, came at 137.87; the text's own sign of error (after 128) was met.

*Behind it, a false assumption*: "VectorE loses 15 low-part subtractions, [...] so it has more air". Some 6.6 us of subtractions went before the table. Against them stood: the five statistics, 4.3 us, that ran from 21.1 to 25.4 behind the centring, where the kernel before had done the same five by 17.2 between its other waits; the addition with a scale, 0.75 instead of 0.66 us; and eight operations slowed by 1 us each, against one before. How much of the delay each of these makes up was not measured one by one; e5 shows that the order alone is worth 7.1 us at the gathers. I had read the windows of VectorE only as a mean over the projection, and it was at 18.3 of 20 us already from 40 to 60.

*Start, +5.4*: measured +7.0, inside the bounds 3 to 8. The four sums took 6.1 us, not 5.1 (the same instructions took 4.98 in e1 and 5.13 in e3), but of that only 0.3 was left at the low part of tile 1 (21.14, forecast 20.8). Most of the rest is in the mask's work, forecast to end at 27.6 and ended at 28.85. One of its three sums met POOL's low part of tile 3 (26.83 to 28.09) and took 1.21 us instead of 0.21:

```profile
L1027 DVE TENSOR_TENSOR_SCAN cum_f<-one_row,part_f x3: 210/211/1206, 27.0 to 28.4; 128x26 f32<-128x26 f32 x3
```

The wait was 4.2 on the mask's totals, as forecast, with the clock falling behind it. e5 shows that 6 us of the 7.0 were a matter of order alone.

*Transposes and waits, -13.2*: from tile 3 to tile 26 the same steps give -12.2 (11 sets of transposes, 5.4, and the waits, 6.8); measured -8.8. The three waits went, as forecast, but VectorE put shorter ones in their place. e9 and e10 show 4.3 us for the second layout where the table is early.

*POOL at the end, +2.0 with bounds 0 and 4*: mechanism right, size wrong. The low part of tile 27 was waited for by 3.7 us, the normalized rows by 2.4, and each was followed by a spell of low clock, about 1.8 us. The sum had POOL's chain from a table 10 us too early. e1 prices the three late low parts at some 2 us of the way to the feed-forward.

*The port, 0*: I looked for it in six scan rows, and case 3 gave it 3 us there. The six scan rows were hardly touched: 4.5 us together, 4.1 before. It was the operations on 8 to 32 columns that I had costed at nothing, because they take 0.2 us. The Trainium skill, "SBUF — State Buffer", section "SBUF: two separate sides", describes an exclusive lock that the later instruction waits for in full; the trace agrees, with 0.17 us become 1.22 for an operation on two SBUF inputs (L1098). What it cost the kernel is not shown: e8, which puts such meetings back, has the feed-forward 0.7 us later.

*The rivals*: case 4 did not happen; POOL scaled the first context row at 39.64, right behind a low part and without a wait. Its sign was right, for another cause. The loss that did happen, a late table, was not among the cases. Its 4.7 us (interval 3.1 to 5.7) lie close to the 4.3 that part slower from same, and 0.13 for slower was too little.

*Held fixed*: the feed-forward groups stayed at 89.9 us. Only group 0 grew, by 1.8 us, where the clock fell behind a carry; the sum had nothing for it.

## What to carry to other kernels

Where a result leaves the fast engine for a table, a store and a gather, that chain has its own clock: follow it back to the queue that starts it, and ask when that queue gets there, not where the step stands in the program. Before taking work off the bounding engine, check that the next one has air in each stretch, not on average: here VectorE was full from 40 to 100 us, and the late table behind it hid the gain. A gap that a change opens in an engine's queue (VectorE waiting for the sums) is a place for work that is ready: filling it gave 7 us (e5), more than the 4.7 that the change itself cost. And work that is moved out of one wait may meet another: the low parts of the weights, moved behind the scale in e6, made the operations of the normalization nearly three times as long.

## What the runs showed of the hardware

- Eight VectorE operations of 8 to 32 columns that started while POOL ran a 128x512 subtraction, addition or multiplication took 1.2 us instead of 0.2, to the end of the POOL instruction. One with a single SBUF operand did so too (L1101 above, 1.20 us), and so did the normalization of 128x512 (L1130 in e6, 1.5 us instead of 0.54). Additions with a PSUM operand did not: 0.75 us in each case. Nor did the second step of the statistics (L981, 128x6 to 128x2, both in SBUF): 0.18 us each time.
- The granted clock fell four times in the kernel after, and not once past the start in e7. Each fall costs about 1.8 us (the clock's mean over 20 us is 0.91), on top of the waits of 2.1 to 4.2 us that it came behind. A wait of 1.8 us before the carry of group 0 left the clock up in the kernel before, e5, e7 and e13; one of 1.9 in e8 and of 2.1 in the kernel after did not, and what follows the first feed-forward matmul is 1.8 to 2.3 us longer there.
- A gather lands long after it is issued: in e6 POOL starts the four 1.85 to 2.1 us apart, and the last landed 7.5 us after its start (107.11 to 114.60).
